# A four-block sequence kernel: row maxima written already negated in the window layers, and key strips of the causal stage transposed two steps earlier

## The reference

```python
x = layernorm(x + retention(x))          # L0_attn, x is (4, 512, 128), 16 heads
x = layernorm(x + window_stack(x))       # L0_ffn, 2 layers, below
x = layernorm(x + causal_attention(x))   # L1_attn, 16 heads of 8, full causal softmax over 512
x = layernorm(x + gated_mlp(x))          # L1_ffn

# one layer of window_stack: 8 heads of 64, window 64 with a look-back of one window
q, k, v = split(shift_token(x) @ wqkv)
q, k = rotary_xpos(l2norm(q) * qs, l2norm(k) * ks)
sim  = where(mask, -big, (8 * q) @ k_lookaround.T)
attn = softmax(sim)                      # exp(sim - max(sim)) / sum
x    = x + (attn @ v_lookaround) @ wo
x    = x + gated_gelu_ffn(layernorm(shift_token(x)))
```

## Times and profile before

| | us |
|---|---|
| runs shown | 1230.69, 1264.14, 1235.23 |
| median of them | 1235.23 |
| profiled execution, device time | 1237.87 |
| its span, first to last instruction | 1236.2 |
| mean granted TensorE clock | 0.856 of full speed |

### The profile page before, as it was taken

One profiled execution on the slowest core, in us unless ns is written; L12 is line 12 of the kernel. 1 busy time (PEld: TensorE's weight loads), 2 busy tenths in 40 slices (PEclk: granted clock), 3 DMA queues, 4 the chain that ended last, 5 costly groups with the idle time before them and its releaser, 6 DMA issues.

```text
span 1236.2 us, 19068 instructions
## 1 busy us (share of the span) xinstructions
PE 997.8 (81%) x6640; PEld 615.3 (50%) x6640; DVE 728.7 (59%) x1882; ACT 546.5 (44%) x1234; POOL 447.9 (36%) x457
## 2 busy tenths in 40 slices
PE   6998698879875777899479986988798757778994
PEld 3666376547642444444336663765476424444443
DVE  4676598579765654330346765985797656543303
ACT  3740465466532554541046404654665325545410
POOL 2244486168450322200122444861684503212001
PEclk9886799999895698799888867999998956987997
DMA  8000110011000000000100001100110000000001
GB/s 350 1 1 0 26 25 15 1 31 27 6 1 1 1 2 1 1 1 1 34 3 2 1 0 27 23 15 1 31 27 6 1 0 1 2 1 1 1 1 34
DMA packets 11631, 21.62 MB, mean 17 GB/s; under 512 B 1424, under 2 KB 6928, under 8 KB 11024
## 3 DMA queue, kind: packets, MB, share of 16 engines
q1 hardware_dynamic: 11248, 18.60, 5.1%
q10 hardware_dynamic: 288, 1.79, 0.4%
HBM read 11.87 MB, written 1.05 MB: 10 GB/s over the span
## 4 chain that ended last, share of the span: by engine, by line
PE 60%; DVE 22%; issue 6%; ACT 5%; POOL 5%; DMA 1%; POOLq 1%; SPq 0%; DVEq 0%; ACTq 0%
PE bank L362 10%; PE bank L759 9%; PE bank L411 5%; PE bank L396 5%; PE bank L456 4%; PE bank L680 4%; DVE arena L1134 3%; PE bank L523 2%; PE bank L647 2%; PE bank L749 2%; DVE arena L1035 2%; DVE arena L1036 2%; PE bank L666 2%; PE bank L578 2%; PE bank L634 2%
## 5 line engine op out<-in xcount | busy, mean ns | idle before, releaser
L362 PE MATMUL bank<-consts_sb,arena 128*128 128x128 f32 x960 | 155.1, 311 | 73.2 <-DVE arena L1126 26.1
L1247 ACT ACTIVATE arena<-bank 128x512 f32<-128x512 f32 (+2 forms) x284 | 136.9, 550 | 169.6 <-PE bank L362 137.8
L362 PEld LDWEIGHTS bank<-consts_sb,arena 128*128 128x128 f32 x960 | 125.1, 160 | 134.3 <-issue 76.2
L1134 DVE TENSOR_REDUCE arena<-bank 128x2 f32<-128x1024 f32 (+3 forms) x128 | 98.1, 819 | 105.2 <-PE bank L634 105.2
L1518 POOL TENSOR_TENSOR rstd<-vareps,neghalf 128x1 f32<-128x1 f32 x96 | 54.2, 565 | 265.9 <-DVE vareps L819 265.1
L1611 POOL TENSOR_SCALAR_AFFINE_SELECT arena<-arena 128x256 f32<-128x256 f32 x128 | 51.5, 416 | 219.7 <-ACT arena L1429 217.4
L1555 POOL TENSOR_TENSOR arena<-arena,neghalf 128x16 f32<-128x16 f32 x32 | 93.0, 2906 | 91.2 <-DVE arena L995 91.2
L456 PE MATMUL bank<-weights,x_features 128*128 128x512 f32 x192 | 102.9, 656 | 20.6 <-DVE arena L1008 8.6
L759 PE MATMUL bank<-arena,weights 128*128 128x512 f32 x256 | 111.9, 594 | 1.6 <-ACT arena L1485 1.6
L1356 ACT ACTIVATE arena<-bank,arena 128x128 f32<-128x128 f32 x256 | 70.6, 371 | 86.9 <-DVE arena L1036 86.9
L1429 ACT ACTIVATE arena<-bank 128x1024 f32<-128x1024 f32 (+1 forms) x96 | 81.8, 882 | 45.8 <-PE bank L666 45.3
(11 more groups left out here) (165 smaller groups left out, 1840.1 us busy)
## 6 DMA issues: line engine op xcount, KB each, us to landing
arena<-arena SPq DMA_DIRECT2D x56, 130.0 KB, 2.3
weights<-wts_dram SPq DMA_DIRECT2D x1, 2824.0 KB, 19.4
weights<-wts_dram SPq DMA_DIRECT2D x1, 1817.0 KB, 13.5
weights<-wts_dram SPq DMA_DIRECT2D x1, 1561.0 KB, 9.6
x_tokens<-x_dram SPq DMA_DIRECT2D x6, 256.0 KB, 3.0
consts_sb<-consts_dram ACTq DMA_DIRECT2D x1, 1232.5 KB, 7.0
out_dram<-x_inner SPq DMA_DIRECT2D x16, 64.0 KB, 1.5
consts_sb<-consts_dram SPq DMA_DIRECT2D x1, 768.0 KB, 4.7
```

The costliest lines, as they stand in the source:

```text
L362: mm = pe.transpose(bank[:, i * P:(i + 1) * P], src, ident)
L1134: ins = dve.tensor_reduce(mx3[:, u % 2, t, 2 * p:2 * p + 2], scores[:, :, at:at + (t + 1) * P], AX, ALU.max)
L1247: return act.activation(dst, src, ACT.Copy)
```

## The change

Two edits. In the window layers the maximum and its negation become one instruction: the reduction takes `negate=True` and writes the bias itself, and the intermediate tile and the wait between the two go. In the causal stage the key strips of unit u+1 are transposed and copied in step 3u instead of step 3u+2; `k_strips` gains a wait for `strips_ready`, since it no longer stands behind `q_strips` of the same unit. Everything else is unchanged. Lines of the changed kernel are shifted by one at most.

```diff
-        K_AT = {NG * u + 2: u + 1 for u in range(G - 1)}
+        K_AT = {NG * u: u + 1 for u in range(G - 1)}
...
                 def k_strips(u):
+                    pe.wait_ge(strips_ready, NT * (u // 4 + 1))
                     bank = take(pe, ("kS", u), [(kS_ready, u + 1)], bank=6)
...
-                            mx = a2["mx"][:, 4 * c:4 * c + 4]
-                            link(dve.tensor_reduce(mx, scores, AX, ALU.max))
-                            dve.tensor_scalar(a2["nb"][:, 4 * c:4 * c + 4], mx, -1.0, None, ALU.mult)\
+                            dve.tensor_reduce(a2["nb"][:, 4 * c:4 * c + 4], scores, AX, ALU.max, negate=True)\
                                 .then_inc(shift_ready, 1)
```

## The result

| | before | changed |
|---|---|---|
| median of four runs, us | 1235.28 | 1198.75 |
| lowest to highest | 1230.69 to 1264.14 | 1195.57 to 1203.17 |
| ratio, 95% interval | 1 | 0.9719 (0.9672 to 0.9765) |
| profiled execution's span | 1236.2 | 1193.9 |
| mean granted clock | 0.856 | 0.870 |

The account below looks back on a forecast made before the run. VectorE was taken to bound full window steps at 10.5 us, and a chain of hand-overs the causal stage. Gains of 20.4 + 12 = 32.4 us off 1237.9 gave 1205.5, adjusted to 1204 us, range 1190 to 1218.

Parts of the forecast that it names:

- Rival C: Causal stage: clock stays at its lower level in units that ran at the upper, 43 us slower, 1247 us; chance 0.04.
- What bounds a full step, and what frees it: Window layers: VectorE bounds full steps at 10.5 us; without L1036 and its contention they take 9.42, gaining 1.05 us.
- handed back: Window full step: of 1.65 us freed on VectorE, L824 beside GpSimd takes back about 0.6, 0.3 less and 0.9 more.
- rival A: Window layers: contention passes on in full to L824, a step gains only about 0.4 us, total 1214; chance 0.13.
- 4.5 + 5.7: Window layers: gain in us of an iteration's two layers from edit 1, counted over early, full and eighth steps and tail.
- the step on L1568: Window eighth step: q transposes wait for GpSimd's L1568, whose chain the freed VectorE time moves 1.4 to 1.5 us earlier.
- The assumption that the negated reduction costs the same: Window layers: the reduction stays at 0.68 us with negated output, shown by no row; extra cost taken as zero.
- Edit 2, the hand-overs: Causal unit starts: removed waits and moved transposes sum to 5.9 us an iteration, about 12 us in all.
- New waits: Causal stage: waits of about 0.7 to 1.0 us before key transposes of steps 0 and 3 and step 18's gather.
- B: Causal stage: edit 2 gains nothing, its time returning as waits in front of L666, total 1217 us; chance 0.11.
- Rival D: Causal stage: one unit more per iteration at the upper clock level, 11 us more gain, 1193 us; chance 0.12.
- 20.4: Window layers: total gain in us forecast for edit 1, the sum of both layers taken for two iterations.

Follow-up runs that it names:

- edit 1 alone: Kernel before with only the negated maxima in the window layers, causal stage unchanged: 1226.38 us, ratio 0.9881.
- experiment 3: Kernel before with the negation kept as its own instruction, issued as a length-one reduction with negated output instead of tensor_scalar: median 1230.19 us, four scattered executions.
- edit 2 alone: Kernel before with only the key strips moved two steps earlier, window layers unchanged: 1215.37 us, ratio 0.9841.
- experiment 4: Kernel before with the key strips still in a unit's last step but ahead of the output transposes: 1227.03 us, ratio 0.9946.
- repeat: The changed kernel measured once more, with no further change: 1196.56 us, ratio 0.9704.
- Experiments 2 and 7: 2 is edit 2 alone, 1215.37 us; 7 is changed kernel plus unused matmuls before the first causal unit: nine 1196.48, fourteen 1196.29, with earlier residual sum 1179.86 us.
- best version: Changed kernel with the causal residual sum issued ahead of the maxima and fourteen unused matmuls ahead of the first unit: 1179.86 us, ratio 0.9545.
- Experiment 6: Changed kernel with VectorE's residual sum (L1164) issued ahead of a step's maxima in the four finishing steps: 1192.34 us, ratio 0.9655.

## Why the prediction was right, and where it was short

**The total.** 1204 forecast, 1198.75 measured, inside the range, and faster by over 2% as 0.70 had it. Rival C fell: no unit of the causal stage that ran at the upper level before runs at the lower in the changed kernel. With edit 1 alone one unit of each iteration did, from 435.90 and from 1046.98 us, 17.91 us at 0.62. So its price is real, but not its reason, a new rhythm: this was the causal code of before, and in experiment 3 the same code kept the level.

**What bounds a full step, and what frees it.** Right. The steps are 9.16 and 9.36 us apart; 9.42 was the forecast, 9.2 to 9.6 the bounds, which the shorter just misses. The waits of 0.56 and 0.38 us are gone. The contention does pass on to L825, as one short and one long instance, 0.52 + 1.30 us; before they were 1.17 + 0.30, so 0.35 us is handed back and not 0.6: the second instance rose by 1.0 us (0.9 forecast), but the first fell by 0.65, where the sum had only 0.3. (Its own 0.4 us for that instance meant 0.8 less than 1.17, so the sum did not follow from its reading.) TensorE has no wait for it, so rival A's mechanism exists and costs nothing there. Per iteration 9.7 and 10.2 us with edit 1 alone, against 4.5 + 5.7. The eighth step's tie moved to GpSimd, as the step on L1568 said. The assumption that the negated reduction costs the same held to 3 ns.

**Edit 2, the hand-overs.** Right in the sum: 5.9 us of waits and moved instructions per iteration, and 5.67 us of idle time gone with edit 2 alone. In its parts it is less exact: units 1 to 3, 4 to 6, and 7 and 8 lost 0.85, 4.66 and 0.26 us of idle time, where the forecast had 1.7, 4.2 and 0. New waits of 1.01, 0.78 and 0.78 us stand where they were expected, ahead of the key transposes of steps 0 and 3 and ahead of the gather. In front of L667 TensorE waits 54.7 us for the maxima in all, 50.6 with edit 2 alone, and 51.5 before (L666), so B fell. (B's own 1238 - 20 - 0 is 1218, not 1217.)

**Edit 2, the size.** Short: 12 us forecast, 20 measured. Two terms were mis-sized. A steady unit gained 1.67 us, not 1.41: the first pass and the wait for the first maximum also shrink, by 0.3 us (experiment 4). And the sum kept TensorE's clock as it stood. Units 1 to 3 gained 5.4 instead of 1.7 us with edit 2 alone, and 3.1 to 5.9 in the four causal stages of the changed kernel and its repeat: their mean clock is 0.59 before, 0.69 with edit 2 alone, and 0.61 to 0.74 in those four. The slower unit at 460 went, 1.4 us; at the end of the stage 0.4 to 1.8 us came back. Rival D named this: one unit more an iteration at the upper level, 5.4 us, where edit 2 alone gained 4.24 us of busy time. It belonged into the sum as a term with a range of its own, not beside it with a chance of 0.12. That the total came out near the forecast is partly luck: edit 2 gained 8 us more than its term, and edit 1 alone some 5 less than its 20.4, because the causal stages of its profile were 6.3 us longer through a lower clock, which isn't shown to be the edit's doing. Part of the 36.5 us is then which profiles and executions were drawn: the repeat's profile lasts 1201.5 us, the first one's 1193.9, with the same code.

The Trainium skill (TensorE: Matmul & The Clock Gate, "Part 1") says that the lower level is the default and that activity releases it. Experiments 2 and 7 agree in direction, with the mean clock of a causal stage at 0.73 before, 0.76 with edit 2 alone, and 0.86 and 0.89 in the best version, its 12 us of dummies included. Experiment 6 agrees in one iteration only: at the end of the stage 0.72 became 0.93 in the first, and 0.64 in the second.

## What to carry to other kernels

Compare the least and the greatest duration of small VectorE instructions in SBUF: here a factor of seven between them was GpSimd's work beside them, and an instruction of another kind removed it, at the same count. When a change takes idle time from TensorE in a stage that changes between its two clock levels, the busy time is a term of the sum too, with a range of its own: here it gave 4.2 us an iteration on top of 5.7 with edit 2 alone, and it rose by 4.4 and 4.1 us in a profile whose causal code was untouched. Read a stage in more than one profile before an effect of a few us is put down to an edit. Before a shortened chain is called done, look for the longest wait left in it: here its removal took 1.1 to 3.2 us of idle time, and 5 us of slower matmuls behind it in one iteration of two.

## What was not expected of the hardware

- The same retention code lasts 120.0 to 120.9 or 123.4 to 124.7 us, in either iteration, in the 24 stages of the twelve profiles, with no edit near it and none between 120.9 and 123.4; the busy time goes with it (104.8 and 107.7 us in the two iterations of experiment 6).
- Behind the wait of 2.62 us the transposes take 1.09 us instead of the 0.63 to 0.66 ahead of it; where the wait was gone the clock stayed at 0.93 in three stages and fell in a fourth right behind one of 0.54 us. The same 0.54 us stand in the best version, where the matmuls behind them are at the upper level. The length of one wait doesn't decide it.
- 12.18 us of dummy matmuls at the upper level did not carry it through the three waits of 1.31, 0.78 and 0.73 us ahead of the first unit: in the four stages with 14 of them its first pass took 0.92 us twice and 0.62 or 0.63 twice, and only one of the four units ran at 1.00 throughout.
- A reduction over a length of one with a negated output is a negation in 157 ns that GpSimd never stretched, in 64 of 64 instances.
